# Row sums from ScalarE's exponentials, and value products in two halves, in the latent attention of a mixed kernel

## The reference

```python
q = (x @ Wqa @ Wqb).reshape(b, s, H, D)               # H = 16 heads of D = 8
kv = (x @ Wkva @ Wkvb).reshape(b, s, KVH, D, 2)       # KVH = 4 key/value heads
k, v = (kv[..., 0], kv[..., 1])
q = _rope(q)
k = _rope(k)
g = H // KVH
k = jnp.repeat(k, g, axis=2)
v = jnp.repeat(v, g, axis=2)
scores = jnp.einsum('bqhd,bkhd->bhqk', q, k) * scale
scores = jnp.where(causal[None, None], -jnp.inf, scores)
w = jax.nn.softmax(scores, axis=-1)
out = jnp.einsum('bhqk,bkhd->bqhd', w, v).reshape(b, s, E)
return out @ Wout + bout
```

## Time and profile before

| | us |
|---|---|
| median of 3 runs | 2121.06 |
| their lowest and highest | 2121.06, 2122.04 |
| the profiled execution, its own time | 2123.64 |
| its span on the core | 2121.8 |
| scores of the first sequence start (L1430) | 1782.53 |
| scores of the last quad of the last sequence start | 1984.02 |
| scores of sequences 3, 4 and 5 start (steps 4, 5, 6) | 1859.02, 1886.10, 1913.17 |

### The profile page before, as it was taken

One profiled execution on the slowest core, in us unless ns is written; L12 is line 12 of the kernel. 1 busy time (PEld: TensorE's weight loads), 2 busy tenths in 40 slices (PEclk: granted clock), 3 DMA queues, 4 the chain that ended last, 5 costly groups with the idle time before them and its releaser, 6 DMA issues. The chain is left out here.

```text
span 2121.8 us, 64825 instructions
## 1 busy us (share of the span) xinstructions
PE 1998.5 (94%) x21611; PEld 1398.7 (66%) x21611; DVE 1536.9 (72%) x3516; ACT 1692.7 (80%) x4279; POOL 1455.7 (69%) x1662
## 2 busy tenths in 40 slices
PE   6799999999999999999999999999999998988696
PEld 3566666666666666666666666666666765655486
DVE  7777777777777777777777777777777764788654
ACT  3688888888888888888888888889898985655355
POOL 5777777777777777777777777777777762344343
PEclk9899999999999999999999999999999998999888
DMA  4222232322232222332223232223534242000023
GB/s 110 50 63 64 47 94 58 73 47 63 64 84 62 64 47 64 80 73 59 61 50 91 63 70 51 59 68 80 129 83 97 56 100 84 2 12 12 14 61 107
DMA packets 191396, 138.95 MB, mean 65 GB/s; under 512 B 47758, under 2 KB 183636, under 8 KB 191172
## 3 DMA queue, kind: packets, MB, share of 16 engines
q1 hardware_dynamic: 189028, 133.09, 26.4%
q0 software_dynamic: 2272, 4.72, 0.7%
HBM read 28.36 MB, written 14.96 MB: 20 GB/s over the span
## 5 line engine op out<-in xcount | busy, mean ns | idle before, releaser
L976 ACT ACTIVATE pr<-bank,mx 128x64 f32<-128x64 f32 x1536 | 336.8, 348 | 0.3 <-DVE mx L1079 0.2
L1161 POOL TENSOR_TENSOR qr<-t 128x512 f32<-128x512 f32 x192 | 245.9, 1281 | 119.5 <-DVE t L1059 119.4
L1058 DVE TENSOR_TENSOR t<-bank,rot_t 128x512 f32<-128x512 f32 x384 | 263.0, 685 | 87.9 <-PE bank L813 85.3
L1149 POOL TENSOR_TENSOR qr<-qr,rn 128x512 f32<-128x512 f32 x192 | 200.6, 1045 | 173.3 <-DVE rn L1030 173.3
L1059 DVE TENSOR_TENSOR t<-bank,rot_t 128x512 f32<-128x512 f32 x384 | 261.5, 681 | 0.0
L1164 POOL TENSOR_TENSOR kr<-t 128x512 f32<-128x512 f32 x192 | 245.9, 1281 | 0.1
L1167 POOL TENSOR_TENSOR sqh<-sq 128x512 f32<-128x512 f32 x192 | 245.8, 1280 | 0.0
L938 ACT ACTIVATE sq<-bank 128x512 f32<-128x512 f32 x192 | 114.3, 596 | 158.2 <-DVE t L1059 158.0
L984 ACT ACTIVATE kBD<-bank 64x512 f32<-64x512 f32 x384 | 229.0, 596 | 3.1 <-PE bank L531 0.8
L813 PE MATMUL bank<-wqkv,xs 128*128 128x512 f32 x384 | 207.2, 622 | 10.1 <-issue 3.5
L864 PE MATMUL bank<-kBD,qT 128*32 128x128 f32 x6144 | 207.5, 276 | 0.4 <-ACT bank L918 0.3
(11 more groups left out here) (256 smaller groups left out, 4337.1 us busy)
## 6 DMA issues: line engine op xcount, KB each, us to landing
vBD<-vS SPq DMA_DIRECT2D x1152, 64.0 KB, 2.0
vBD<-vS SPq DMA_DIRECT2D x576, 32.0 KB, 1.8
wqkv<-in_L_ffn_Wqkv_dram SPq DMA_DIRECT2D x12, 768.0 KB, 6.5
rows<-const SPq DMA_DIRECT2D x4, 2244.0 KB, 11.0
wo<-in_L_ffn_Wo_dram SPq DMA_DIRECT2D x12, 256.0 KB, 2.9
t<-rows SPq DMA_DIRECT2D x39, 66.0 KB, 1.8
vBD<-in_L_ffn_W_dram SPq DMA_DIRECT2D x1, 2048.0 KB, 8.6
vBD<-in_L_ffn_W_dram SPq DMA_DIRECT2D x8, 256.0 KB, 7.0
```

Source lines behind the costliest of these rows:

```text
L976: ins = act.activation(pr[:, slot % 2, hd, :], bank[5][:, hd * 64:(hd + 1) * 64], ACT.Exp, bias=mx[:, slot % 2, hd:hd + 1])
L1058: dve.tensor_tensor(t1[:, m], src, tab[:, 0, :].unsqueeze(1).broadcast_to([P, HH, DH]), ALU.mult)
L1149: pool.tensor_tensor(x, x, rn[:, slot, half * HH:(half + 1) * HH].unsqueeze(2).broadcast_to([P, HH, DH]), ALU.mult).then_inc(norm.sem, 1)
L1161: pool.tensor_tensor(qr[:, slot].rearrange("p (h d) -> p h d", d=DH), t1[:, 0], t2[:, 0], ALU.add).then_inc(q_add.sem, 1)
```

## The change

Four things change, all inside the latent attention.

- **Sums.** The exps write their row sums to `csum` as an accumulator output. `conesb` and its products are gone: 16 of the 32 products of a `values` call. In their place VectorE takes the reciprocal of the 128x32 sums at the end of quad 2, GpSimd spreads it over 256 columns (`cinx`, which lies in wo), TensorE turns these 128x256 in quad 0 of the next step (two transposes into the second half of bank 2), ScalarE copies them to `crd`, and VectorE only multiplies (`normalise_values`). The multiplication now stands between the two copies of quad 0.
- **Halves.** `values` of quads 0 and 1 run in two halves: one where it was, one between the turns of r = 1 and r = 2. The projection of the values (L1506, now L1551) moves behind the turns of r = 0 and 1. `values` of quad 2 stay together in quad 0 of the next step.
- **Second home.** Turned probabilities go to two homes in turn, vS and a part of attT with gs.
- **Order.** ScalarE's first exp of quad 0 stands ahead of the copies instead of behind the gate's. On VectorE `add_stream` moves from between the two copies of quad 0 to behind both.

```diff
-        conesb = sb("conesb", [P, GRP, 32])
         cnb = sb("cnb", [P, KVH, GRP])
+        csum, cinv = sb("csum", [P, NT, KVH, GRP]), sb("cinv", [P, NT * QH])
+        cinx = wo[:, :, :].rearrange("p c d -> p (c d)")[:, 0:SEQ]
 
...
         cp = qr[:, :, :]
-        cpT = [vS[:, r].rearrange("p e q d -> p (e q d)") for r in range(KVH)]
+        late = attT[:, :, :].rearrange("p c k -> p (c k)")
+        cpT = [[vS[:, r].rearrange("p e q d -> p (e q d)") for r in range(KVH)],
+               [late[:, 512 * k:512 * (k + 1)] for k in range(1, KVH)] + [gs[:, :, :].rearrange("p c k -> p (c k)")[:, 0:512]]]
         cvj = sq[:, :, :].rearrange("p h d -> p (h d)").rearrange("p (k r j x) -> p k r j x", k=NT, r=KVH, j=GRP)
...
-            def turns(a, m, g):
-                for r in range(KVH):
+            def turns(a, m, g, rs):
+                for r in rs:
                     G = NG * a + KVH * m + r
                     pe.wait_ge(c_exp.sem, c_exp.after(G))
+                    if a and (m, r) == (0, 0):
+                        pe.wait_ge(c_keep.sem, c_keep.after(a - 1))
...
-            def values(a, m):
+            def values(a, m, part):
...
-                for x in range(4):
+                for x in (0, 1) if part == 0 else (2, 3):
                     j, kb = j0 + x // nk, x % nk
-                    for o, ones in ((0, False), (SEQ, True)):
-                        for r in range(KVH):
-                            mm = pe.matmul(bank[1][32 * r:32 * r + 32, o + t * P:o + (t + 1) * P],
-                                           conesb[:, j, :] if ones else cvj[:, kb, r, j, :], cpT[r][:, x * P:(x + 1) * P],
-                                           start=(m == 0 and x == 0 and not ones), stop=(x == 3), skip_group_check=True)
-                mm.then_inc(c_o.sem, 1)
+                    for r in range(KVH):
+                        mm = pe.matmul(bank[1][32 * r:32 * r + 32, t * P:(t + 1) * P], cvj[:, kb, r, j, :],
+                                       cpT[n % 2][r][:, x * P:(x + 1) * P], start=(m == 0 and x == 0), stop=(x == 3),
+                                       skip_group_check=True)
+                if part:
+                    mm.then_inc(c_o.sem, 1)
 
...
+                        if live(2):
+                            pe.wait_ge(c_pta.sem, c_pta.after(2 * (NQ * c + 2) + 1))
+                            pe.wait_ge(c_nrm.sem, c_nrm.after(c, 2))
+                            for t in range(NT):
+                                mm = pe.transpose(bank[2][:, SEQ + t * P:SEQ + (t + 1) * P],
+                                                  cinx[:, t * P:(t + 1) * P], ident)
+                            mm.then_inc(c_back.sem, 1)
                         if live(3):
-                            n = NQ * c + 2 if live(2) else NQ * NB - 1
-                            pe.wait_ge(c_pta.sem, c_pta.after(2 * n + 1))
+                            if not live(2):
+                                pe.wait_ge(c_pta.sem, c_pta.after(2 * (NQ * NB - 1) + 1))
                             choose_turn(pe, s - 3, 1 - par)
                         if live(2):
-                            values(c, 2)
-                        if live(1):
-                            if live(0):
-                                pe.wait_ge(ln_tok.sem, ln_tok.after(LN_C + s))
-                            for t in range(NT):
-                                mm = pe.matmul(high[:, t * 32:(t + 1) * 32], ckva[:, t * P:(t + 1) * P], wvb[:, :], start=True, stop=True)
-                            mm.then_inc(c_pv.sem, 1)
+                            values(c, 2, 0)
+                            values(c, 2, 1)
...
-                            values(a, 0)
+                            values(a, 0, 0)
...
-                            values(a, 1)
+                            values(a, 1, 0)
...
                     if live(1):
-                        turns(a, m, s - 3 if live(3) else None)
+                        turns(a, m, s - 3 if live(3) else None, (0, 1))
+                        if m:
+                            values(a, m - 1, 1)
+                    if m == 0 and live(1):
+                        if live(0):
+                            pe.wait_ge(ln_tok.sem, ln_tok.after(LN_C + s))
+                        for t in range(NT):
+                            mm = pe.matmul(high[:, t * 32:(t + 1) * 32], ckva[:, t * P:(t + 1) * P], wvb[:, :], start=True, stop=True)
+                        mm.then_inc(c_pv.sem, 1)
+                    if live(1):
+                        turns(a, m, s - 3 if live(3) else None, (2, 3))
...
-                        act.activation(cpT[r], bank[2][:, :], ACT.Copy).then_inc(c_pta.sem, 1)
+                        act.activation(cpT[(NQ * a + m) % 2][r], bank[2][:, :], ACT.Copy).then_inc(c_pta.sem, 1)
...
-                                ins = act.activation(cp[:, r, hh * n:(hh + 1) * n], bank[4 + r][:, hh * n:(hh + 1) * n],
-                                                     ACT.Exp, bias=cnb[:, r, hh:hh + 1])
+                                ins = act.activation(cp[:, r, hh * n:(hh + 1) * n], bank[4 + r][:, hh * n:(hh + 1) * n], ACT.Exp,
+                                                     bias=cnb[:, r, hh:hh + 1], accum_out=csum[:, t, r, j0 + hh:j0 + hh + 1])
                             ins.then_inc(c_exp.sem, 1)
+                        if r == 0 and m == 0 and live(2):
+                            act.wait_ge(c_back.sem, c_back.after(s - 2))
+                            if live(3):
+                                act.wait_ge(g_back.sem, g_back.after(s - 3))
+                            act.activation(crd, bank[2][:, SEQ:2 * SEQ], ACT.Copy).then_inc(c_keep.sem, 1)
+                        if r == 0 and m == 0 and live(3):
+                            act.wait_ge(g_back.sem, g_back.after(s - 3))
+                            act.wait_ge(d_lmm.sem, d_lmm.after(s - 4))
+                            act.activation(xnG, bank[2][:, 0:SEQ], ACT.Copy).then_inc(g_out.sem, 1)
...
+            def normalise_values(a):
+                dve.wait_ge(c_o.sem, c_o.after(NQ * a + 2))
+                dve.wait_ge(c_keep.sem, c_keep.after(a))
+                dve.tensor_tensor(con, bank[1][:, 0:SEQ], crd, ALU.mult).then_inc(c_nrm.sem, 1)
...
-                            dve.tensor_copy(cpT[r], bank[3][:, :]).then_inc(c_ptd.sem, 1)
-                            if m == 0 and r == 1 and live(-1):
-                                add_stream(dve, s + 1)
-                    elif m == 0 and live(-1):
+                            dve.tensor_copy(cpT[(NQ * a + m) % 2][r], bank[3][:, :]).then_inc(c_ptd.sem, 1)
+                            if m == 0 and r == 1 and live(2):
+                                normalise_values(c)
+                    elif m == 0 and live(2):
+                        normalise_values(c)
+                    if m == 0 and live(-1):
                         add_stream(dve, s + 1)
+                    if m == 2 and live(1):
+                        dve.wait_ge(c_exp.sem, c_exp.after(NG * a + NG - 1))
+                        dve.reciprocal(cinv[:, :], csum[:, :, :, :].rearrange("p t r j -> p (t r j)")).then_inc(c_nrm.sem, 1)
...
+                if live(1):
+                    pool.wait_ge(c_nrm.sem, c_nrm.after(s - 1, 1))
+                    if s > 1:
+                        pool.wait_ge(c_back.sem, c_back.after(s - 2))
+                    pool.tensor_copy(cinx.rearrange("p (h d) -> p h d", d=QD), cinv[:, :].unsqueeze(2).broadcast_to([P, NT * QH, QD])).then_inc(c_nrm.sem, 1)
```

More of the change, by code:

```diff
@@ L318, in mixed_kernel @@
         c_pta, c_ptd = sig("c_pta", credit=6), sig("c_ptd", credit=6)
-        c_vz, c_one = sig("c_vz"), sig("c_one")
-        c_o = sig("c_o")
-        c_nrm = sig("c_nrm", per=2, credit=2)
+        c_vz = sig("c_vz")
+        c_o, c_back, c_keep = (sig(x) for x in ("c_o", "c_back", "c_keep"))
+        c_nrm = sig("c_nrm", per=3, credit=2)
         c_y, c_res = sig("c_y"), sig("c_res", credit=3)
@@ L1552, in lat_act @@
                     t, j0, nh, nk = QUADS[m]
-                    if m == 0 and live(3):
-                        act.wait_ge(g_back.sem, g_back.after(s - 3))
-                        act.wait_ge(d_lmm.sem, d_lmm.after(s - 4))
-                        act.activation(xnG, bank[2][:, 0:SEQ], ACT.Copy).then_inc(g_out.sem, 1)
                     if m == 2 and live(0):
```

12 lines of the change are left out of this document (removed).

## The result

| | before | changed |
|---|---|---|
| median, us | 2121.43 (4 runs, 2121.06 to 2122.04) | 2147.48 (4 runs, 2147.05 to 2149.41) |
| ratio to before | 1 | 1.0121, 95% interval 1.0109 to 1.0134 |
| the profiled execution, and its span | 2123.64, 2121.8 | 2149.41, 2147.6 |
| first scores to last scores of the attention | 201.49 | 228.86 |
| last scores to the end of the span | 137.78 | 137.78 |

The changed kernel is slower, 26.05 us by the medians; 15.7 were predicted. All of it lies in the attention: +27.4 us between the first scores row and the last. The first scores themselves start 1.6 us earlier, at 1780.96, in code that is the same, and what follows the last scores is as long as before.

What follows compares the result with a forecast made beforehand. ScalarE was taken to bound quad 0 and quad 1 of steps 1 to 3, VectorE quad 2 and full steps' quad 1. 13.0 + 4.6 - 1.9 = +15.7 us on 2123.64, less 2.6, gave 2136.8; range 2119 to 2160.

Steps and rivals of the forecast that it cites:

- e: ScalarE's price per exp for the accumulator output, taken as 0.11 us; 14.1 us over the 128 exps of quad 0.
- the clock: TensorE's granted clock, 1.00 before; a fall below 1.00 with less work on TensorE was costed at nothing.
- Rival A: The accumulator on ScalarE's exps is free: -1.0 us, 2120.0, not slower; chance 0.15.
- rival B: ScalarE reads each sum behind the finished exp, 0.2 to 0.31 us each: 2155.0 to 2183; chance 0.25.
- Quad 0, order: Quad 0's first exp starts 2.38 us after the scores, not 3.26; with two copies behind, -0.32 us in steps 4 to 7.
- Quad 1: `add_stream` delays the maxima 0.32 us in steps 1 to 6, +1.9; with the accumulator's cost there, +4.6 us.
- The tail: Step 9, without exps: the long reciprocal and products go, the new chain gives about 0.8 back; -1.9 us.
- Products removed, cost nothing: Removing half the value products takes 22.7 us of TensorE's work, hidden behind ScalarE's exps, so no change in time.
- Rival C: The relieved engine bounds the attention: 2098.4 us if TensorE, 2109.8 if VectorE; chance 0.05.
- Halves, second home: Moving 0.47 us of products between turns fills a wait, and the second home removes no visible wait: costed at nothing.
- Rival D: GpSimd's spreading comes over 1 us late and holds quad 0: 7 us per us late, around 2145; chance 0.05.
- full step of 28.8 us: Sign expected in the profile after: a full attention step lasts about 28.8 us instead of 27.08.

Runs made afterwards that it cites:

- no_accum_fill: Changed kernel without the accumulator output on its exps, plus unread products in TensorE's waits of quads 0 and 2; ratio 0.9987 to the kernel before.
- after_fill: Changed kernel plus unread products in TensorE's waits of quads 0 and 2, nothing left out; ratio 1.0069 to the kernel before.
- no_ones: Kernel before without the products against `conesb`, its reciprocal reading a table instead; ratio 1.0039 to the kernel before.
- accum_only: Kernel before with only the accumulator output added to each exp, its sums unread; ratio 1.0130 to the kernel before.
- ones_kept: Changed kernel with the products against `conesb` put back behind the value products, unread; ratio 1.0158 to the kernel before.
- order_only: Kernel before with quad 0's first exps ahead of the gate's copy and VectorE's multiplication between its two copies; ratio 0.9980 to the kernel before.
- no_accum: Changed kernel without the accumulator output on its exps, the sums set to constants; ratio 1.0012 to the kernel before.
- order_warm: Same as order_only, plus unread products in TensorE's waits behind the attention; ratio 0.9987 to the kernel before.

## Why the prediction was right, and where it was not

Direction and range were right, and so was the main mechanism: the price e of an accumulator, on ScalarE's path, in quad 0 above all. The size was 26 instead of 15.7, and the step that failed is the one costed at nothing: the clock. The stages of four traces add up to the whole: no_accum_fill against before -2.45, reads (after_fill against no_accum_fill) +13.54, clock (changed against after_fill) +16.28, together +27.37. The first term is not clear of chance: 1.66 of the 2.45 us lie in step 1, where the kernel before has two scores rows of 1.90 and 1.69 us.

That 15.7 came as near as it did is in part luck. Its terms for the attention were 13.0 + 4.6 = 17.6 us; with the clock mostly held (after_fill against before) they measure 11.1. What was put too high made up for a part of the 16.3 us that were missing.

- *e = 0.11.* Measured 0.09 by starts and 0.084 by quads (9.88 - 8.53 = 1.35 for 16). The path had the right exps on it: from no_accum_fill to after_fill the quads 0 grow by 10.7 us and the quads 1 by 2.2, together 12.9, where 16.7 were predicted and 152 x 0.084 give 12.8. The other 0.6 of the 13.54 us is clock: quad 2 of step 2 lasts 9.78 us in after_fill, 8.21 in no_accum_fill, and quad 2 of step 4 9.78 in no_accum_fill, 8.88 in after_fill. It is a small instruction of its own that overlaps its neighbours, the case the forecast took. Rival A (free) and rival B (0.2 and more) fall by the same row.
- *Quad 0, order.* Predicted -0.32 in steps 4 to 7, measured 9.03 to 8.53, -0.50. The first exp started at 2.23, not 2.38: I had charged VectorE's small reciprocal with its duration, 0.35 (0.34 measured), but the next instruction starts 0.26 after it, and the maxima lost 0.02 us.
- *Quad 1.* `add_stream` was put at 0.32 and cost 0.16, by the same mistake: its neighbour starts 0.33 behind it, not 0.41, and L418 left 0.16 of slack, not 0.09 (0.68 us from its start to the maxima's, where 0.52 do). Half of 1.9 us. That 8 exps of 0.09 vanish in the 0.86 us of slack of the full steps was right: 9.32 with reads (after_fill) and without (no_accum_fill).
- *Quad 2.* 8.88 and 8.89 where the clock is full, as predicted.
- *The tail.* Predicted -1.9. In no_accum_fill -1.4, 12.11 against 13.52 us from the last scores to the gate's bias; in the changed kernel -0.5. The products ahead (L1469, L1474 in no_accum_fill) take 0.43 us in both, so their clock does not explain the 0.9 us between the two; 0.6 of it arises before them (they start 10.18 and 9.55 us after the last scores), and the cause is open. To the end of the span nothing is left of it: 137.78 us before and after.
- *Products removed, cost nothing.* They were hidden, as predicted, and that did not make them free to remove: no_ones is 0.39% slower (0.25 to 0.53), with the lower clock in three stretches. Rival C, and the Trainium skill's rule behind it (Perfetto Trace Analysis, Identifying the Most-Contended Engine), fall: VectorE was relieved of 11.7 us and TensorE's loads fell too, and the kernel got slower. The cleaner case is no_accum_fill, where ScalarE gets no reads: VectorE has 12.7 us less to do (1524.2 against 1536.9), and the kernel is 0.13% (2.8 us) faster, where rival C had 11.3 or 22.7.
- *Halves, second home.* Nothing at full clock, as predicted. The homes were not tried apart.
- *Rival D.* The spreading is in time in every full step, no row waits for it; in step 9 it is 0.19 us late.

The full step of 28.8 us that was to show each step right is there, 28.85 in step 5, but by chance: quad 1 holds 0.76 us of the clock's loss, and at full clock (after_fill) the step is 28.08. Step 6, at 32.55, is what the prediction did not have.

What is shown is that filling TensorE's waits restores the clock and 11 us of time at unchanged reads, and that reads alone or removed products alone bring it down. That the longer waits in quad 0 are the cause in the changed kernel itself is argued from these. The sums of the listed waits in quad 0 of step 5 speak for it in most traces: 2.65 us in the changed kernel, 2.60 in accum_only, 2.36 in no_ones and 1.76 in ones_kept, where the clock falls in three to nine stretches; 1.43 in the kernel before, 1.30 to 1.32 in the four kernels with fills and reads, and 0.65 in order_only, with none to two. But no_accum, with 1.37 us, has six stretches below 1.00, and no_ones, with 2.36 in every full step, only three, all before step 4. So the length of these waits goes with the clock and does not alone decide it, and ones_kept and order_warm show that the amount of work does not either.

## What to carry to other kernels

An accumulator output is not free: count one small instruction per ACTIVATE, 0.08 to 0.09 us here, and multiply by those on the path, which for the many short exps here (1.35 us in a quad 0) is more than the products that it replaces (0.945 us, and hidden). Before taking hidden work off TensorE, or lengthening its waits, look at how steady its granted clock is; price the case in which it falls from a row at either level (here 1.14 and 2.09 us for a quad's scores). And add up starts, not durations, on engines whose rows overlap.

## What the runs showed that I had not expected

- Many waits of about 1 us, inside a stage whose TensorE is busy 16 of 20 us, go with the lower clock: in quad 0 of step 5 of the changed kernel the longest listed wait is 0.84 us, the longest of the step 1.22, and the scores behind quad 0 took 1.95 us. The Trainium skill (TensorE: Matmul & The Clock Gate, A second HAM failure mode: psum-queue depth-cycling) says that frequent short idle times between groups of products make the clock swing between its two levels; the traces here agree.
- A kernel of more work was faster: after_fill, with 16 more products in each full step, by 11 us. And less work was slower: no_ones, by 0.39%, of which 3.8 us stand in the stage.
- A half clock can also stand over TensorE's unbroken work: 4.00 of 4.00 us busy at 0.50 in order_warm, twice in a row, after a wait of 1.83 us.
- The reads and the clock do not add in step with the number of half-clock stretches: accum_only has five, the changed kernel nine, at nearly the same stage (226.68 and 228.86).
